# Two small awaited memsets on POOL behind every second gather of the graph attention

## The reference, cut to what matters

```python
h = (x_flat @ W_gat).reshape(M, HEADS, NUM_EXPERTS)        # 4 heads x 4
a_src = (h * att_src).sum(-1); a_dst = (h * att_dst).sum(-1)
e = leaky_relu(a_src[src] + a_dst[dst])                    # one per edge and head
ee = exp(e - segment_max(e, dst)[dst])
alpha = ee / segment_sum(ee, dst)[dst]
agg = segment_sum(h[src] * alpha, dst)                     # 16 numbers per node
scores = layernorm(agg + b_gat).mean over heads            # 4 per node -> top 2 -> softmax -> gates
out = sum over experts e of gate_e * (gelu(x @ W1[e] + b1[e]) @ W2[e] + b2[e])
```

## Time and profile before

| what | value |
|---|---|
| median of three runs | 4632.89 us (4626.37 to 4638.28) |
| the profiled execution | 4626.74 us, its span 4624.8 us |
| mean granted clock of PE | 0.886 |
| busy: PE, DVE, ACT, POOL | 3742.1, 2236.7, 1346.1, 672.0 us |
| POOL's gathers, L2327 | 256 in all, 1004 and 1003 ns each |

### The profile page before, as it was taken

One profiled execution on the slowest core, in us unless ns is written; L12 is line 12 of the kernel. 1 busy time (PEld: TensorE's weight loads), 2 busy tenths in 40 slices (PEclk: granted clock), 3 DMA queues, 4 the chain that ended last, 5 costly groups with the idle time before them and its releaser, 6 DMA issues. The chain is left out here.

```text
span 4624.8 us, 91402 instructions
## 1 busy us (share of the span) xinstructions
PE 3742.1 (81%) x23942; PEld 2677.0 (58%) x23943; DVE 2236.7 (48%) x5781; ACT 1346.1 (29%) x2980; POOL 672.0 (15%) x1160
## 2 busy tenths in 40 slices
PE   4888865799789989985193677959989899799998
PEld 2444433566478669753082555649879444457776
DVE  7888878888810121143072455160220777623333
ACT  2555532677710110231010022330000135233333
POOL 3222100000000000014605222000000466100000
PEclk9999975778799899997596788979999999889999
DMA  2111220222134115202111131224335100100000
GB/s 105 47 72 75 91 93 0 84 89 91 71 141 170 56 71 202 82 14 54 14 49 33 18 33 56 95 98 180 129 112 207 35 1 1 16 18 7 14 14 28
DMA packets 124630, 319.58 MB, mean 69 GB/s; under 512 B 42658, under 2 KB 74897, under 8 KB 109228
## 3 DMA queue, kind: packets, MB, share of 16 engines
q1 hardware_dynamic: 111332, 302.42, 18.7%
q0 software_dynamic: 9760, 8.89, 1.9%
q10 hardware_dynamic: 3404, 6.53, 0.4%
HBM read 245.52 MB, written 72.43 MB: 69 GB/s over the span
## 5 line engine op out<-in xcount | busy, mean ns | idle before, releaser
L557 PE MATMUL ps<-hot_key,hot_src 128*126 128x512 bf16 (+1 forms) x2208 | 416.9, 314 | 39.7 <-DVE hot_key L522 20.8
L522 DVE TENSOR_SCALAR hot_key<-col_iota,run_keys 128x625 bf16<-128x625 int16 x1104 | 394.0, 379 | 0.0
L1338 PE MATMUL ps<-gnn_u_thirds,near 125*128 125x256 bf16 x3000 | 337.2, 275 | 22.3 <-issue 22.3
L557 PEld LDWEIGHTS ps<-hot_key,hot_src 128*126 128x126 bf16 x2208 | 212.7, 136 | 235.4 <-DVE hot_key L522 172.5
L1338 PEld LDWEIGHTS ps<-gnn_u_thirds,near 125*128 125x128 bf16 x3000 | 331.1, 141 | 27.1 <-issue 24.3
L2490 PE MATMUL ps<-table_thirds,rows_room 125*128 125x144 bf16 x2304 | 173.7, 232 | 199.1 <-issue 181.0
L2490 PEld LDWEIGHTS ps<-table_thirds,rows_room 125*128 125x128 bf16 x2304 | 154.4, 100 | 221.7 <-issue 219.1
L2446 PE MATMUL ps<-xnT,ew 128*128 (+2 forms) x640 | 206.5, 475 | 80.0 <-issue 48.5
L519 DVE TENSOR_SCALAR hot_src<-col_iota,run_srcs 128x125 bf16<-128x125 int16 x828 | 211.8, 256 | 98.4 <-PE ps L557 49.6
L866 PE MATMUL ps<-row_hot,slot_hot 128*128 128x512 f16 x1088 | 223.7, 359 | 1.5 <-DVE row_hot L1079 1.0
L3640 DVE SCALAR_TENSOR_TENSOR xres<-ps,shares,xres 125x256 f32 x200 | 96.8, 484 | 241.7 <-PE ps L3605 220.8
(11 more groups left out here) (570 smaller groups left out, 6853.9 us busy)
## 6 DMA issues: line engine op xcount, KB each, us to landing
near<-adjacency SPq DMA_DIRECT2D x80, 1562.5 KB, 6.5
adjacency<-counts SPq DMA_DIRECT2D x125, 312.5 KB, 2.2
own_in<-own_rows SPq DMA_DIRECT2D x34, 512.0 KB, 4.0
expert_rows<-rows_y SPq DMA_DIRECT2D x75, 125.0 KB
rows_room<-expert_rows SPq DMA_DIRECT2D x25, 375.0 KB
pair_in<-high_rows SPq DMA_DIRECT2D x34, 256.0 KB, 4.8
pair_in<-low_rows SPq DMA_DIRECT2D x34, 256.0 KB, 5.3
rows_room<-key_rows SPq DMA_DIRECT2D x8, 1024.0 KB
```

The costliest lines, as they stand in the source:

```text
L522: nc.vector.tensor_scalar(hot_key[:, j, :], col_iota[:], run_keys[:, ds(at, 1), j:j + 1].rearrange("p a j -> p (a j)"), None, ALU.is_equal ...
L557: last = nc.tensor.matmul(sums[:, b:e], hot_src[:, j, :], hot_key[:, j, b:e], start=False, stop=True, skip_group_check=True)
L1338: last = nc.tensor.matmul(ps[:, j, 0:width], lead_tiles[BUF[j]][:, k, :], parts.thirds[:, k, i, :], start=(k == 0 and i == 0), stop=(k == ...
```

## The change

`gather_rows` gets a call behind every second gather. `rest(n)` has POOL write zeros into a tile of one number per partition, wait for the write to be finished, and do both once more. POOL executes in order, so the first wait is over only when the two gathers ahead of the memset have been issued as well. With 256 gathers there are 128 rests: 256 memsets and 256 waits. Nothing else is altered, and nothing reads the tile.

```diff
+                    rested = sem("att_rested")
+                    idle = s("att_idle", [128, 1])
...
                             for j in range(first, stop):
                                 pool.indirect_dma_start(
                                     out=fetched[q][:, j, :], out_offset=None, in_=node_table,
                                     in_offset=bass.IndirectOffsetOnAxis(ap=src_idx[:, q, j:j + 1], axis=0),
                                     bounds_check=N - 1, oob_is_err=False).then_inc(got[q], 16)
+                                if j % 2:
+                                    rest(b * (SLOTS // 2) + (j // 2 - SLOTS))
+
+                        def rest(n):
+
+                            for k in range(2):
+                                nc.gpsimd.memset(idle[:], 0.0).then_inc(rested, 1)
+                                alone(pool, rested, n * 2 + (k + 1))
```

## The result

The changed kernel took **4438.41 us** (median of 4 runs, 4434.07 to 4442.45) against 4635.59 us (4 runs, 4626.37 to 4640.67) of the kernel before beside it: ratio 0.9574, 95% interval 0.9555 to 0.9592, 4.3% faster. The forecast was 4449 us. Its profiled execution took 4442.14 us with a span of 4440.2 us, 184.6 us less than the profiled execution of before. A *sitting* is a group of runs made one after another on one chip. In another sitting (e5) the same edit made the kernel 2.6% slower; the experiments come to that. The *hold* is the state that the prediction starts from: PE and DVE hardly move while POOL issues gathers.

What follows compares the result with a forecast made beforehand. Piled-up gathers were taken to hold PE; with rests POOL becomes the bound. At 3.85 us a pair, block 3's `weigh` starts at 2641.5 instead of 2818.8 us: 4626.7 less 177.3 gives 4449 us, range 4400 to 4675.

Steps and rivals of the forecast that it cites:

- Pile-up holds PE, and rests empty it: Gathers issued every 1.30 us but served at 1.40 pile up and hold PE; 3.85 us a pair frees it; chance 0.67.
- first 9 us: Start of block 2's gathers: PE runs as ever, so a run's first eight gathers, 1.30 us apart, do not hold it.
- PE loses 310 us: Over three stretches of gathers: PE could reach block 3's `weigh` at 2509 us, where it happens at 2818.8.
- The pair, 3.85 us: On POOL, two gathers plus one rest of two awaited memsets take 3.85 us, where a pair took 2.60.
- the lower bound of 3.54: Low case for a pair on POOL, without the 0.30 us gap behind a gather: 3.54 us, giving 4410 us.
- 4.58: High case for a pair on POOL, if the second memset needs a gather's 0.92 us start: 4.58 us, giving 4543 us.
- POOL becomes the bound: With PE free, POOL's order sets the stretch up to block 3's `weigh`, which starts at 2641.5 instead of 2818.8 us.
- The 25 transfers keep their hold: The 25 transfers at L2353 get no rests, so their small hold on PE stays.
- Rival 1: No relief: the hold lasts while gathers are issued at all, so rests make it 156 us slower, 4783 us; chance 0.19.
- Rival 2: Each gather blocks PE for 1.40 us, leaving it 1.05 of 3.85 us, 27%: 4671 us, slower; chance 0.14 with any share.

Runs made afterwards that it cites:

- e5: The changed kernel once more, unchanged, in a sitting without the hold: 4414.04 us against 4303.27 us of the kernel before, ratio 1.0256.
- e9: Kernel before with each gather split into two of 64 rows, 512 transfers instead of 256, in a sitting with the hold: 4982.85 us.
- e11: Changed kernel's rest only behind every eighth gather, in a sitting with the hold: 4543.53 us against 4626.36 us of the kernel before.
- e1: Kernel before plus one memset behind every second gather, waited for only two rests later; no hold in that sitting: 4301.26 us against 4300.86.
- e2: Changed kernel's rest only behind every fourth gather, in a sitting without the hold: 4354.99 us, ratio 1.012 to the kernel before.

## Why the prediction was right, and what it did not see

- **Pile-up holds PE, and rests empty it** (0.67): right in what it forecast, PE free and POOL the bound; the mechanism behind it holds in part only. Its rows show PE in stretches of 72 at 2157.85 (forecast 2162), the gather's end at 2256.2 (2254), block 1's start at 2308.1 (2306) and end at 2407.7 (2397). The last is the largest miss: block 1's gather took 99.6 us and not 91.7. e9 shows the 1.40 us per transfer directly. Two things go against a plain queue served at 1.40. In e11, with 0.05 us of room in 1.45 and never more than 0.7 us of pile, PE was still held for the most part. And the kernel before is held from its fifth gather on. The prediction read its first 9 us as free, though rows 1 have PE busy for 6.36 of them, and took from this that eight gathers hold nothing. With two gathers between rests that misreading did no harm. How much room is needed, between 0.05 and 0.47 us a gather, was not measured.
- **PE loses 310 us:** about right. The kernel before takes 4626 to 4636 us with the hold and 4293 to 4303 without, some 330 us less. Where they lie is read from e1's trace, which has the time of the kernel before without the hold: block 3's `weigh` is at 2523.4 instead of 2818.8, 295 us earlier, and behind it stand 4298.4 - 2523.4 = 1775.0 us instead of 4624.8 - 2818.8 = 1806.0, 31 us less. The 295 answer to the 310, and e1's `weigh` waits 5 us of the difference for DVE. That is a stand-in: the kernel before was not traced without the hold.
- **The pair, 3.85 us:** the one term that was mis-sized. A clean pair takes 3.51: the gap of 0.30 us behind an indirect DMA does not exist ahead of a memset, which is the lower bound of 3.54. (The prediction's own terms add up to 3.56 there, and to 4.62 where it has 4.58; both slips are under 0.05 us.) The second memset waited 0.15 us, the gather behind it 0.85 (0.16 and 0.92 assumed). Longer gathers and a few pauses of POOL bring the mean of block 2's 64 pairs to 3.76: from 2134.13 to the end of the last rest at 2373.78, and 0.85 for the next start, are 240.5 us. All 128 pairs took 479.8 us where the forecast had 492.8, 13.0 less. A start 1.1 us late, 0.2 more at the two seams between the stretches, 0.3 for the last rest, which takes 1.22 us and not 1.55 of the time that is counted off, and 0.7 more from the last gather to `weigh` give 2.3 back. Left are 10.7 us: `weigh` at 2630.8, forecast 2641.5.
- **POOL becomes the bound:** right. Neither store waits for sums, ACT stands for 105 us and PE for 108.
- **The 25 transfers keep their hold:** right, 3.4 us beyond the kernel before's. 188.0 - 3.4 = 184.6 us, forecast 177.3.
- **Rival 1** (hold while gathers are issued at all) falls with the window of 149.6 us, and not by the first 9 us that the prediction held against it. **Rival 2** (PE runs only in the free part) falls too on the result: PE is busy for 93% of 161 us, and the free part would be 27% or, at 1.87 us a gather, 25%. In e11, with 3% of free part, PE does a third of its work: more than that rule gives, so it doesn't hold there either.
- **What the prediction took for granted,** and the runs refute, is that the kernel before always has this hold. Without it there is nothing to win, and the rests lengthen POOL's order, the bound of the stretch: +110.8 us (the prediction's sum for this, rival 1's, has 156), which is the "rests would only lengthen POOL's stretches" that the prediction set beside the Trainium skill's "SBUF — State Buffer", section "SBUF: two separate sides". e1 agrees with that section (PE 153 of 161 us busy beside the gathers), the kernel before with the hold does not (39 of 161). That the forecast came out is luck in this one respect: the comparison fell in a sitting with the hold, as three of eight did.
- **Open:** what decides whether a sitting has the hold; what stands in line at 1.40 us per transfer, since the data doesn't; and whether e1's short lead, or a rest behind every fourth gather, would lift the hold. The last two met no sitting with it, so whether rests work by the room they leave, by the short queue, or by the memset itself is not shown. In those without it, e1 costs nothing and e2 1.2%.

## What to carry to other kernels

When an engine crawls at one instruction per transfer of another engine's stream and the program has no wait there, space the stream out and look whether the crawl goes. For a price of 1.40 us a transfer, 1.87 us with an awaited pause behind every second one freed PE here, and 1.45 us with a pause behind every eighth did not. Count what the spacing costs where that stream becomes the bound: here 0.87 us for each rest, all of it at the end. And measure such a remedy in several sittings before it is kept: this one changes the time by -4.3% in one and +2.6% in another.

## What the runs showed of the hardware beyond what was expected

- The same kernel took 4293 to 4303 us in five sittings (medians) and 4626 to 4636 us in three, without mixing within one (the longest has 16 runs, all at 4292.06 to 4307.22), and chips of the same number showed both.
- With the hold and transfers back to back, PE gets one instruction in 1.40 us, whether a transfer has 128 rows or 64. It begins after five gathers in the kernel before, and goes on up to 27 us after POOL's last one (e9), though the queue's packets end within about 3 us of the last gather of the kernel before.
- Without it, 89 gathers 1.34 us apart cost PE nothing that shows (e1: busy for 153.3 of 161 us; e5, 1.87 us apart: 152.3). The gathers are themselves longer beside busy engines: 59 of 256 took over 1.1 us in e1 and 39 in the changed kernel, up to 3.3 us, against 6 in the kernel before with PE and DVE held.
- A memset on POOL starts at the end of the indirect DMA ahead of it (0.00 us), while an indirect DMA behind another starts 0.30 us later, and one behind an awaited memset 0.85 us later.
